# Layer 0's experts on tokens sorted by expert in DRAM, instead of every expert on every token

## The chip, the cores and the metric

The kernel runs on one NeuronCore of a Trainium2 chip. TensorE (PE) multiplies, VectorE (DVE), ScalarE (ACT) and GpSimd (POOL) work element by element, and SyncE (SP) issues nearly all DMAs. Every engine runs its own instructions in order, and waits for the others on semaphores. The metric is the device time in microseconds, lower is better.

## What is computed

A two-layer network on x of shape 16 batches x 256 tokens x 128 channels, all float32. Layer 0 is a recurrent mixer and an MLP, and then a mixture of 8 experts; layer 1 is an attention and then a mixture of 4 attention experts. Only layer 0's experts change:

```python
probs = softmax(x @ Wg)                      # 8 experts
top_vals, top_idx = top_k(probs, 2)          # two per token
top_vals = top_vals / sum(top_vals)
h = relu(einsum('ebsd,edh->ebsh', x * mask, W1) + b1)     # 128 -> 256
y = einsum('ebsh,ehd->ebsd', h, W2) + b2                  # 256 -> 128
out = sum(y * scores, axis=expert)           # scores are 0 but for two experts
x = layernorm(x + out)
```

## The kernel before

All engines walk the same list, `program_order()` (L272). First layer 0: 8 chunks of 512 tokens (two batches, 4 tiles of 128 rows), as steps (c, i) with i from 0 to 15. The chunks are pipelined by hand: in iteration c the mixer of chunk c+2, the MLP of chunk c+1 and the experts of chunk c run. Its iterations go from -2 to 8 (L276). Then follow the periods r of layer 1 with 24 slots each: -6 to 17 (L279). Periods -6, -5 and -4 hold only the projections and norms of the first batches (called the preparation here); from r = -3 (`EARLY_PERIODS`) the scores, maxima and exponentials of layer 1 start. Layer 1's large buffers lie over those of layer 0, so at (-3, 0) POOL, ACT and DVE wait until layer 0 has its last output (`x4_ready`, L961, L1079, L1356).

In layer 0's iteration c the work that matters here is, by the step's number:

- i = 0: DVE forms x1 of chunk c+1 (L561, L564) from the mixer's product; ACT sums its squares (L461), POOL takes the inverse root at i = 1 (L386, L388), DVE scales (L568, i = 2), PE transposes, ACT copies (i = 3).
- i = 4 to 9: the MLP of chunk c+1: PE multiplies by `wfc` (L698), ACT halves (L471), DVE takes the maximum (L611), ACT squares (L475), PE multiplies by `wmlp` (L704).
- i = 10 to 15: DVE adds and takes the norm's sums of chunk c+1 (L572 to L577), POOL the root, DVE writes x3 (L580, helper L518), PE transposes it and multiplies by `wg`. In between, the mixer of chunk c+2: transposes, k, v, the scan (L543), `wkv` (L547), the gate by exp, add, and two reciprocals (L551 to L554), `mixT` (L555), and PE's product with `wo0` (i = 15).
- i = 0 and 1: DVE picks the two best experts of each token of chunk c (L614 to L625).
- Experts, dense: each of the 8 on all 512 tokens. `hidden_at` and `output_at` place them: two products of 512 columns by `w1` (L650), ACT's relu with bias (L428), eight products of 128 columns by `w2` (L659), and DVE adds the output times the token's score (L596). All weights stay in SBUF.

A float32 product is two PE instructions in the trace; `mm` is the helper at L634.

SP loads everything at the start (`loads`, L370) and has no work in layer 0 after that. In layer 1 it issues small DMAs (`attention_sync`).

Of the kernel before, what the change touches and what calls it, by code (L numbers as in the profile page):

```python
# [28 lines left out]
STEPS, LAST_STEPS = 16, 6  # L29
# [22 lines left out]
class LayerZeroSignals:  # L52


    def __init__(self, sem):
# [11 lines left out]
        self.state_ready = sem("state_ready")  # L67
        self.mixT_ready = sem("mixT_ready")
        self.mix_ps = sem("mix_ps")
        self.mix_used = sem("mix_used")  # L70
# [18 lines left out]
        self.lg_copied = sem("lg_copied")  # L89
        self.lg_ready = sem("lg_ready")  # L90
        self.pexp_ready = sem("pexp_ready")
        self.score_ready = sem("score_ready")
        self.scoreT_ps = sem("scoreT_ps")
        self.scoreT_ready = sem("scoreT_ready")
        self.b2_ps = sem("b2_ps")
        self.b2_used = sem("b2_used")
        self.hidden_ps = sem("hidden_ps")
        self.hidden_ready = sem("hidden_ready")
        self.y_ps = sem("y_ps")
        self.y_used = sem("y_used")  # L100
        self.acc_sums = sem("acc_sums")
        self.acc_rstd = sem("acc_rstd")
        self.x4_ready = sem("x4_ready")
        self.dve_step = sem("dve_step")
        self.pool_step = sem("pool_step")
# [79 lines left out]
def program(nc, a, out):  # L185
    with ExitStack() as ctx:
# [8 lines left out]
        x4_all = sb("x4_all", [P, B * T, D])  # L195
# [26 lines left out]
        ew_ready = sem("ew_ready")  # L222
        exp_decay = sem("exp_decay")
        x_first = sem("x_first")
        x_loaded = sem("x_loaded")
# [4 lines left out]
        z = LayerZeroSignals(lambda name: sem(f"{name}_l0"))  # L230

# [40 lines left out]
        def program_order():  # L272

            for c in range(-2, CHUNKS + 1):  # L276
                for i in range(STEPS if c < CHUNKS else LAST_STEPS):
                    yield True, c, i
            for r in range(FIRST_PERIOD, B + 2):  # L279
                for i in range(SLOTS):  # L280
                    yield False, r, i

        with ExitStack() as ph:
            def sb0(name, shape, dt=F32):
# [7 lines left out]
            w1 = sb0("w1", [D, E0, HB * P])  # L292
            b1 = sb0("b1", [P, E0, HB])
            w2 = sb0("w2", [P, E0, HB, D])
            b2 = sb0("b2", [E0, D])
# [6 lines left out]
            x_all = sb0("x_all", [P, B * T, D])  # L302
# [3 lines left out]
            var0 = sb0("var0", [P, 4, CT])  # L306
            rstd0 = sb0("rstd0", [P, 4, CT])
            bn60 = sb0("bn60", [P, 2, CT, 6])
            mv0 = sb0("mv0", [P, 2, CT, 2])
# [4 lines left out]
            er = sb0("er", [D, CS])  # L314
# [10 lines left out]
            x3 = sb0("x3", [P, CT, D])  # L325
            acc = sb0("acc", [P, 2, CT, D])
            h_moe = sb0("h_moe", [P, 2, HB, CS])
            lg0 = sb0("lg0", [P, CT, E0])
            pr0 = sb0("pr0", [P, CT, E0])
            oh1 = sb0("oh1", [P, CT, E0])  # L330
            oh2 = sb0("oh2", [P, CT, E0])
            tk = sb0("tk", [P, CT, E0])
            st0 = sb0("st0", [P, 7, CT])
            score = sb0("score", [P, CT, E0])
            scoreT = sb0("scoreT", [E0, CS])
            hidden_bank = [ps[:, 0:2, :], ps[:, 2:4, :]]
            y_bank = [ps[:, 4, :], ps[:, 5, :]]
# [8 lines left out]
                (w1[:], a["w1"].rearrange("e i o -> i e o")), (b1[:], a["b1"].rearrange("e (c p) -> p e c", p=P)),  # L346
                (w2[:], a["w2"].rearrange("e (c p) d -> p e c d", p=P)), (b2[:], a["b2"]),
# [5 lines left out]
            def chunk(k):  # L353
                return 0 <= k < CHUNKS

            def hidden_at(c, i):

                if i % 2 == 0:
                    return None
                k, e = (c + 1, 0) if i == 15 else (c, (i + 1) // 2)  # L360
                return (k, e) if chunk(k) else None

            def output_at(c, i):

                if i % 2:
                    return None
                k, e = (c - 1, 7) if i == 0 else (c, i // 2 - 1)
                return (k, e) if chunk(k) else None

            def loads(sp):  # L370
# [4 lines left out]
                sp.dma_start(x_all[:, CT:B * T, :], x_rows[:, CT:B * T, :]).then_inc(x_loaded, DMA)  # L375
                for dst, src in loads0:
                    sp.dma_start(dst, src, allow_slow_non_contiguous=True).then_inc(loaded0, DMA)
# [1366 lines left out]
```

## Time and profile before

| | |
|---|---|
| median of 3 runs | 1551.77 us (1539.64 to 1557.17) |
| the profiled execution | 1544.68 us, its span 1542.9 us |
| PE, share of the span | 85% |
| DVE | 66% |
| ACT | 50% |
| POOL | 34% |
| mean granted clock of TensorE | 0.911 |

The span goes from the first instruction to the last. A busy share is a mean over stages that have different limits, so what one stage is worth is read from its own stretch. A gap is named by what ended it. The granted clock is a share of 2.4 GHz and has two levels, 1.2 and 2.4 GHz; a value between them is a mean over a stretch.

### The profile page before, as it was taken

The page shows a single profiled execution, that of the slowest core. Times are in us where ns is not written, and L with a number is a line of the kernel's source. Part 1 is how long each engine was busy: PE and PEld are TensorE (multiplying, and loading weights), DVE is VectorE, ACT ScalarE, POOL GpSimd, SP SyncE. Part 2 cuts the span into 40 slices and gives each one's busy share as a digit, 9 for nine tenths or more (in the row PEclk, how much of TensorE's full clock was granted, in tenths as well). Part 3 has the DMA queues.
Part 4 walks back from the last instruction along what each step waited for, and adds up shares of the span by engine and source line. Part 5 has one row for each costly group of instructions (what it writes and reads, how often), then busy time and mean ns, then how long its engine had stood idle before and what let it go on. Part 6 is the DMA issues. An engine that isn't in the chain of part 4 may idle for free.

```text
span 1542.9 us, 31463 instructions
## 1 busy us (share of the span) xinstructions
PE 1311.5 (85%) x12320; PEld 786.5 (51%) x12320; DVE 1017.0 (66%) x2422; ACT 767.9 (50%) x1260; POOL 525.6 (34%) x863
## 2 busy tenths in 40 slices
PE   4899999999655879889888899998989989988884
PEld 1566666667422335455445555555545545554543
DVE  3677667775444667777687777777777767757520
ACT  3334444433132356566465665665655656653540
POOL 1000010100342235346354454453544542442421
PEclk7999999999755879899899999999999999999986
DMA  7000000000000000101101011011010110110111
GB/s 206 1 1 1 1 1 1 0 1 1 0 1 9 9 2 9 38 11 33 31 13 42 18 26 37 8 42 31 13 42 5 39 36 9 42 36 10 32 34 36
DMA packets 34730, 35.03 MB, mean 23 GB/s; under 512 B 20070, under 2 KB 28440, under 8 KB 32536
## 3 DMA queue, kind: packets, MB, share of 16 engines
q1 hardware_dynamic: 34584, 33.03, 9.1%
q8 instruction: 99, 1.62, 0.5%
q14 instruction: 47, 0.39, 0.1%
HBM read 28.93 MB, written 2.88 MB: 21 GB/s over the span
## 4 chain that ended last, share of the span: by engine, by line
PE 44%; DVE 28%; SPq 7%; ACT 7%; POOL 5%; issue 5%; DMA 3%; DVEq 0%; ACTq 0%; POOLq 0%
PE ps L1367 17%; PE ps L634 14%; DVE mneg_e L1191 7%; PE ps L1445 7%; SPq L832 3%; PE ps L1468 3%; SPq L828 2%; DVE mneg_l L1191 2%; DVE acc L596 2%; DMA sums_l<-o_l 1%; SPq L850 1%; ACT probs L1038 1%; POOL q_low L915 1%; DMA sums_e<-o_e 1%; DVE equal L1217 1%
## 5 line engine op out<-in xcount | busy, mean ns | idle before, releaser
L1038 ACT ACTIVATE probs<-ps 128x1024 f32<-128x1024 f32 x384 | 389.8, 1024 | 244.9 <-PE ps L1367 243.9
L1191 DVE TENSOR_REDUCE mneg_e<-ps 128x2 f32<-128x512 f32 x512 | 337.1, 685 | 64.3 <-PE ps L1367 61.4
L1367 PE MATMUL ps<-k_high,q_high 32*128 32x256 f16 x1024 | 160.5, 283 | 50.6 <-DVE mneg_e L1191 41.3
L1191 DVE TENSOR_REDUCE mneg_l<-ps 128x2 f32<-128x512 f32 x256 | 167.8, 682 | 53.9 <-PE ps L1367 52.3
L1367 PE MATMUL ps<-q_high,k_high 32*128 32x256 f16 x1024 | 141.3, 276 | 4.1 <-ACT probs L1038 3.5
L1445 PE MATMUL ps<-probs,v_e 128*32 128x256 f32 x2048 | 138.6, 389 | 6.7 <-ACT v_e L1063 4.6
L1367 PE MATMUL ps<-q_low,k_high 32*128 32x256 f16 x1024 | 140.4, 273 | 0.0
L1367 PE MATMUL ps<-q_high,k_low 32*128 32x256 f16 x1024 | 139.6, 271 | 0.0
L428 ACT ACTIVATE h_moe<-ps,b 128x512 f32<-128x512 f32 x128 | 81.0, 684 | 116.9 <-PE ps L634 116.9
L634 PEld LDWEIGHTS ps<-w,h_moe 128*128 128x128 f32 x1024 | 122.1, 192 | 16.9 <-issue 16.7
L634 PE MATMUL ps<-w,h_moe 128*128 128x128 f32 x1024 | 124.6, 275 | 0.0
L634 PE MATMUL ps<-x3T,w 128*128 128x512 f32 x256 | 123.7, 606 | 0.0
L1367 PE MATMUL ps<-kT,qT 32*128 32x256 f16 x512 | 76.0, 290 | 33.2 <-DVE mneg_e L1191 17.0
L991 POOL TENSOR_TENSOR on_e<-o_e,on_e 128x512 f32<-128x512 f32 x64 | 80.6, 1272 | 62.5 <-DMA on_e<-scratch_e 62.5
L1367 PEld LDWEIGHTS ps<-k_high,q_high 32*128 32x128 f16 x1024 | 53.8, 93 | 93.9 <-DVE mneg_e L1191 62.1
L1246 DVE SCALAR_TENSOR_TENSOR q<-ps,bq,pick 128x256 f32<-128x256 f32 x128 | 55.6, 476 | 55.6 <-PE ps L1367 33.7
L1367 PE MATMUL ps<-wo,on_e 128*128 128x128 f32 x512 | 89.5, 346 | 0.0
L1367 PEld LDWEIGHTS ps<-q_high,k_high 32*128 32x128 f16 x1024 | 48.6, 93 | 77.4 <-issue 49.4
L921 POOL CAST k_high<-k 128x512 f16<-128x512 f32 x64 | 39.5, 618 | 139.0 <-ACT k L1054 139.0
L1367 PEld LDWEIGHTS ps<-wo,on_e 128*128 128x128 f32 x512 | 82.3, 252 | 4.5 <-issue 1.5
L1445 PEld LDWEIGHTS ps<-probs,v_e 128*32 128x32 f32 x2048 | 54.1, 110 | 58.6 <-issue 21.7
L1367 PE MATMUL ps<-x5T,wq 128*128 128x256 f32 x256 | 72.4, 405 | 5.7 <-ACT k L1054 4.9
(216 smaller groups left out, 2393.6 us busy)
## 6 DMA issues: line engine op xcount, KB each, us to landing
on_e<-scratch_e SPq DMA_DIRECT2D x64, 256.0 KB, 4.6
on_l<-scratch_l SPq DMA_DIRECT2D x128, 32.0 KB, 1.9
sums_l<-o_l SPq DMA_DIRECT2D x128, 2.0 KB, 1.7
q_high<-shiftT_e SPq DMA_DIRECT2D x128, 2.0 KB
sums_e<-o_e SPq DMA_DIRECT2D x128, 4.0 KB, 1.7
out<-y SPq DMA_DIRECT2D x16, 128.0 KB, 2.0
w<-in_w SPq DMA_DIRECT2D x1, 1024.0 KB
qT<-shiftT_l SPq DMA_DIRECT2D x64, 2.0 KB
```

The costliest lines, as they stand in the source:

```text
L428: last = act.activation(h_moe[:, e % 2, n, :], hidden_bank[e % 2][:, n, :], ACT.Relu, bias=b1[:, e, n:n + 1])
L596: last = v.scalar_tensor_tensor(acc[:, k % 2, t, :], y_bank[e % 2][:, t * D:(t + 1) * D], score[:, t, e:e + 1], base[:, t, :], ALU.mult, A ...
L634: return pe.matmul(o, l, r, start=start, stop=stop)
L832: sp.dma_start(sums_l[row:row + PACK, :], o_l[row:row + 1, :, :]).then_inc(L.sums_landed, DMA)
L921: pool.tensor_copy(k_high[:, b % 2, g], k32[:, g % 2]).then_inc(s.k16_ready, 1)
L991: pool.tensor_tensor(on_e[:, :, g], o_e[:, :, g], on_e[:, :, g], ALU.mult).then_inc(E.on_ready, 1)
L1038: act.activation(probs[:, probs_slot(r, i)].rearrange("p j s -> p (j s)"), s_banks(i).rearrange("p j s -> p (j s)"), ACT.Exp, scale=0.5 if ...
L1191: v.tensor_reduce(to, tiles(max_bank(k)), axis=AX, op=ALU.max, negate=True).then_inc(kind.max_used, 1)
L1246: last = v.scalar_tensor_tensor(q32[:, g % 2, c, :], x0[:, c * S:(c + 1) * S], bq[:, c, g:g + 1], pick[:, c, :], ALU.add, ALU.mult)
L1367: return pe.matmul(o, l, r, start=start, stop=stop)
L1445: last = pe.matmul(x1[ROW * j:ROW * (j + 1), to * S:(to + 1) * S], values, probs[:, probs_slot(r, first + 2 * t + j // 2), j % 2, c * S:(c ...
L1468: last = pe.matmul(x0[:, c * S:(c + 1) * S], wk[:, c, g, :], x5T[:, b % 2], start=False, stop=True, skip_group_check=True)
```

## The change

Layer 0 is cut into two groups of 4 chunks. The router's choice is turned into a place: a mask of the two chosen experts is multiplied on PE with a triangle of ones (rank within the tile) and with all ones (count of the tile), and DVE adds these to running first rows. POOL then writes every row of x3 twice, by indirect DMA with 128 row numbers, into `by_expert[g]` in DRAM, which has a region for each expert. When a group is complete, DVE makes a table of 40 tiles: first row, and first row of the expert's weights. The experts run over these in 10 quads of 4 tiles. For every tile SP reads row numbers from the table into registers, loads 128 tokens and all of the expert's weights and biases (642 values for each of 128 rows), and stores the 128 outputs over the tokens. Later POOL gathers each token's two outputs, by two indirect DMAs per tile, and DVE adds them to x3 with their shares, and normalizes.

Group 0's quads lie in iterations 4 to 7; group 1's lie after layer 0, beside the preparation and the sums of group 0. The sums of group 1 lie on the odd slots from r = -3 on. DRAM regions are zeroed at the start. Besides this, the gate is a tanh on ACT and one DVE instruction; the mixer's and the MLP's scales are multiplied into the weights once; x1 + x is formed on POOL. The core of the diff:

```diff
-            for c in range(-2, CHUNKS + 1):
-                for i in range(STEPS if c < CHUNKS else LAST_STEPS):
-                    yield True, c, i
-            for r in range(FIRST_PERIOD, B + 2):
+            experts_at = {(4, 8), (4, 13), (5, 2), (5, 7), (5, 12), (6, 2), (6, 7), (6, 12), (7, 1), (7, 5), (7, 9), (7, 13)}
+            n = -1
+            for c in range(-2, CHUNKS):
+                for i in range(STEPS):
+                    yield "layer0", c, i
+                    if (c, i) in experts_at:
+                        yield "experts", 0, n
+                        n += 1
+            prepared = [("attention", r, i) for r in range(FIRST_PERIOD, EARLY_PERIODS) for i in range(SLOTS)]
+            summed = list(sums_of(0))
+            done = 0
+            for n in range(-1, QUADS + 1):
+                yield "experts", 1, n
+                yield from summed[3 * (n + 1):3 * (n + 2)]
+                upto = len(prepared) * max(n, 0) // QUADS
+                yield from prepared[done:upto]
+                done = upto
+            rest = sums_of(1)
+            for r in range(EARLY_PERIODS, B + 2):
                 for i in range(SLOTS):
-                    yield False, r, i
+                    yield "attention", r, i
+                    if i % 2:
+                        yield from itertools.islice(rest, 1)
...
+                sp.wait_ge(set_up, 1)
+                for g in range(GROUPS):
+                    if g > 0:
+                        sp.wait_ge(z.filled, DMA * FILLS * g)
+                    rows_of_group = by_expert[g].rearrange("(p n r) d -> n p (r d)", p=P, n=FILLS)
+                    for n in range(FILLS):
+                        sp.dma_start(rows_of_group[n], zeros).then_inc(z.filled, DMA)
...
+                    if i in (10, 12, 13, 14) and chunk(c):
+                        t = (10, 12, 13, 14).index(i)
...
+                        for n in range(2):
+                            pool.indirect_dma_start(by_expert[g], bass.IndirectOffsetOnAxis(ap=places[:, n, at:at + 1], axis=0),
+                                                    x_all[:, at, :], None).then_inc(z.scattered[g], DMA)
...
+                        for n in range(2):
+                            pool.indirect_dma_start(gathered[:, k % 2, n, t, :], None, by_expert[g],
+                                                    bass.IndirectOffsetOnAxis(ap=places[:, n, k * CT + t:k * CT + t + 1], axis=0))\
+                                .then_inc(ex.gathered[k % 2], DMA)
...
-                    link(v.tensor_scalar(gate[:], er[:], 1.0, None, ALU.add))
-                    link(v.reciprocal(gate[:, 0:S], gate[:, 0:S]))
-                if i == 14 and chunk(k):
-                    link(v.reciprocal(gate[:, S:CS], gate[:, S:CS]))
-                    v.tensor_tensor(mixT[:], wkv[:], gate[:], ALU.mult).then_inc(z.mixT_ready, 1)
+                        v.scalar_tensor_tensor(mixT[:], gate[:], 1.0, wkv[:], ALU.add, ALU.mult).then_inc(z.mixT_ready, 1)
...
+                    if n + 1 < QUADS:
+                        q = QUADS * g + n + 1
+                        take(5, ex.tokens_ready, q + 1)
+                        pe.wait_ge(ex.tokens_loaded[q % 3], DMA * QUAD * (q // 3 + 1))
+                        for j in range(QUAD):
+                            last = pe.transpose(tokens_bank[:, j * P:(j + 1) * P], tokens[:, q % 3, j, :], ident[:])
...
+                        pe.wait_ge(ex.tokens_ready, q + 1)
+                        pe.wait_ge(ex.weights_loaded[q % 3], DMA * QUAD * (q // 3 + 1))
+                        for j in range(QUAD):
+                            for k in range(HB):
+                                last = pe.matmul(hidden_bank[q % 2][:, k, j * P:(j + 1) * P], expert_w[:, q % 3, j, k * P:(k + 1) * P],
+                                                 tokensT[:, q % 2, j * P:(j + 1) * P], start=True, stop=True)
...
+                    if n >= 1:
+                        q = QUADS * g + n - 1
+                        take(4, ex.out_ready, q + 1)
+                        pe.wait_ge(ex.hidden_ready, q + 1)
...
+                def load_weights(g, n):
+                    q = QUADS * g + n
+                    if q > 2:
+                        sp.wait_ge(ex.out_ready, q - 2)
+                    for j, row in enumerate(values(g, 1, n)):
+                        sp.dma_start(expert_w[:, q % 3, j, :], a["expert_w"][bass.ds(row, P), :]).then_inc(ex.weights_loaded[q % 3], DMA)
+                def slot(g, n):
+                    if n == -1:
+                        sp.wait_ge(z.filled, DMA * FILLS * GROUPS)
+                        sp.wait_ge(z.table_ready, g + 1)
+                        load_weights(g, 0)
+                        sp.wait_ge(z.scattered[g], DMA * 2 * CT * GROUP_CHUNKS)
+                        for ahead in range(2):
+                            load_tokens(g, ahead)
+                        load_weights(g, 1)
+                    if n >= 1:
+                        store_outputs(g, n - 1)
+                    if 0 <= n < QUADS - 2:
+                        load_tokens(g, n + 2)
+                    if 0 <= n < QUADS - 2:
+                        load_weights(g, n + 2)
...
+                        for n in range(2):
+                            add = v.scalar_tensor_tensor(x_all[:, token, :], gathered[:, k % 2, n, t, :], shares[:, n, token:token + 1],
+                                                         x_all[:, token, :], ALU.mult, ALU.add)
+                            link(add)
...
                     if (r, i) == (EARLY_PERIODS, 0):
-                        v.wait_ge(z.x4_ready, CHUNKS)
+                        for n in range(2):
+                            v.wait_ge(ex.stored[n], DMA * QUAD * QUADS)
```

In slot n PE transposes the tokens of quad n + 1, makes the hidden product of quad n (8 products of 128 columns) and the output product of quad n - 1 (8 more). ACT copies the transposed tokens and takes 8 relus of 128 columns; DVE adds the bias of the outputs (4 instructions) and signals `out_ready`. `load_tokens` and `store_outputs` on SP are made as `load_weights`: four row numbers read into registers, four DMAs; the store waits for `out_ready` of its quad. In the sums, POOL waits for `ex.stored` (all stores of the group) before the first gather, and DVE for `ex.gathered`.

## Rows read from the trace of the kernel before

**Rows 1.** The page: span, busy time, PE and its clock in 40 slices.

```profile
span 1542.9 us, 31463 instructions
...
PE 1311.5 (85%) x12320; PEld 786.5 (51%) x12320; DVE 1017.0 (66%) x2422; ACT 767.9 (50%) x1260; POOL 525.6 (34%) x863
...
PE   4899999999655879889888899998989989988884
...
PEclk7999999999755879899899999999999999999986
```

**Rows 2.** Groups in layer 0 (0 to 420 us): busy us, mean ns.

```profile
L634 PE MATMUL ps<-w,h_moe 128*128 128x128 f32 x1024 | 124.6, 275 | 0.0
L634 PE MATMUL ps<-x3T,w 128*128 128x512 f32 x256 | 123.7, 606 | 0.0
...
L428 ACT ACTIVATE h_moe<-ps,b 128x512 f32<-128x512 f32 x128 | 81.0, 684 | 116.9 <-PE ps L634 116.9
L596 DVE SCALAR_TENSOR_TENSOR acc<-ps,score,acc 128x128 f32<-128x128 f32 x224 | 62.8, 343 | 12.8 <-PE ps L634 12.0
```

**Rows 3.** Timeline, iterations -2 and -1: start us, us, engine, work.

```profile
20.92 2.04 PE L634 MATMUL ps<-wo,mixT 128*128 128x128 f32 x8 [6.44 <-DVE mixT L555]
...
23.73 0.69 DVE L564 TENSOR_TENSOR x_sb<-tmp,x_all 128x512 f32<-128x512 f32 x1
...
39.04 3.81 PE L634 MATMUL ps<-wmlp,h_fc 128*128 128x128 f32 x32 [2.79 <-ACT h_fc L475]
...
49.05 1.11 DVE L518 TENSOR_SCALAR x<-tmp,mv,rstd 128x128 f32<-128x128 f32 x4
...
50.53 1.75 DVE L552 RECIPROCAL gate<-gate 128x256 f32<-128x256 f32 x1
...
51.70 1.85 PE L634 MATMUL ps<-wg,x3T 128*128 128x8 f32 x8 [0.77 <-ACT x3T L478]
...
59.47 0.69 DVE L564 TENSOR_TENSOR x_sb<-tmp,x_all 128x512 f32<-128x512 f32 x1
```

**Rows 4.** Timeline of iteration 2, with dense experts.

```profile
149.86 0.69 DVE L564 TENSOR_TENSOR x_sb<-tmp,x_all 128x512 f32<-128x512 f32 x1
...
152.13 1.95 PE L634 MATMUL ps<-w,h_moe 128*128 128x128 f32 x16
...
156.75 0.63 PE L638 MATMUL ps<-ident,xn 128*128 128x128 f32 x4 [0.95 <-DVE xn L568]
```

**Rows 5.** Timeline of DVE: x1 of chunk 5 begins iteration 4.

```profile
241.36 0.69 DVE L564 TENSOR_TENSOR x_sb<-tmp,x_all 128x512 f32<-128x512 f32 x1
```

**Rows 6.** DMA GB/s, 40 slices of 0 to 60 us; issues on SP.

```profile
GB/s 0 168 200 41 250 291 307 291 298 287 339 240 30 206 395 411 322 369 382 281 198 0 0 0 0 0 0 0 0 0 0 0 0 5 0 0 0 11 5 0
...
0.73 0.44 SPq L372 DMA_DIRECT2D x_all<-in_x  x1
...
452.75 2.69 SPq L884 DMA_DIRECT2D qT<-shiftT_l  x4
```

**Rows 7.** The page's DMA issues: KB each, us to landing.

```profile
sums_l<-o_l SPq DMA_DIRECT2D x128, 2.0 KB, 1.7
```

**Rows 8.** Timeline of POOL: the root, and slots (-3, 0), (-3, 21), (-2, 21).

```profile
404.39 1.01 POOL L388 TENSOR_TENSOR rstd<-var,half 128x4 f32<-128x4 f32 x1
...
437.57 2.66 POOL L962 MEMSET v_e<- 128x3072 f32 x1
...
455.87 0.72 POOL L996 TENSOR_TENSOR x_all<-x_all,bproj 128x256 f32<-128x256 f32 x1
...
496.18 0.72 POOL L996 TENSOR_TENSOR x_all<-x_all,bproj 128x256 f32<-128x256 f32 x1
```

**Rows 9.** Stretch, length, busy us of PE, PEld, DVE, ACT, POOL; clock, DMA.

```profile
404.00:437.00 33.00, 10.32 (x33) 4.58 (x34) 13.75 (x28) 6.45 (x12) 19.20 (x52) 0.54 0.00 0
...
437.00:458.00 21.00, 13.76 (x60) 4.49 (x58) 13.05 (x23) 4.75 (x9) 9.38 (x21) 0.50 0.00 1
458.00:498.00 40.00, 22.40 (x154) 8.93 (x154) 14.44 (x30) 13.28 (x20) 9.52 (x23) 0.59 0.04 8
```

More of the change, by code:

```diff
@@ L1 @@
+import itertools
 import numpy as np
@@ L576, in slot @@
-                        link(v.tensor_tensor(tmp[:], tmp[:], rows(x_all, k), ALU.add))
-                        sums(0, tmp).then_inc(z.x3_sums, 1)
+                        for t in range(CT):
+                            last = v.bn_stats(bn60[:, t, :], tmp[:, t, :])
+                        link(last)
+                        for t in range(CT):
+                            last = v.bn_aggr(mv0[:, t, :], bn60[:, t, :])
+                        last.then_inc(z.x3_sums, 1)
                     if i == 12 and chunk(k):
@@ L626, in slot @@
-                    if i == 2 and chunk(c - 1):
-                        sums(1, acc[:, (c - 1) % 2]).then_inc(z.acc_sums, 1)
+                        if c == 0:
+                            v.wait_ge(const_ready, 7)
+                        first_largest(pr0[:], st0[:, 3, :], chosen[:, 0])
+                    if i == 1 and chunk(c):
+                        link(v.scalar_tensor_tensor(lg0[:], chosen[:, 0], -2.0, pr0[:], ALU.mult, ALU.add))
+                        first_largest(lg0[:], st0[:, 4, :], chosen[:, 1])
+                        v.tensor_tensor(mask[:], chosen[:, 0], chosen[:, 1], ALU.add).then_inc(z.mask_ready, 1)
@@ new lines, in layer0_vector, with experts_vector, slot @@
+                return slot
+            def experts_vector(v):
+                def slot(g, n):
+                    if n >= 1:
+                        q = QUADS * g + n - 1
+                        v.wait_ge(ex.out_ps, q + 1)
+                        if q > 1:
+                            v.wait_ge(ex.stored[q % 2], DMA * QUAD * (q // 2))
+                        for j in range(QUAD):
+                            b2 = expert_w[:, q % 3, j, EXPERT_COLS - D:EXPERT_COLS]
+                            last = v.tensor_tensor(y_tokens[:, q % 2, j, :], out_bank[:, j * D:(j + 1) * D], b2, ALU.add)
+                        last.then_inc(ex.out_ready, 1)
+                return slot
@@ L1078, in slot @@
                     if (r, i) == (EARLY_PERIODS, 0):
-                        act.wait_ge(z.x4_ready, CHUNKS)
+                        for n in range(2):
+                            act.wait_ge(ex.stored[n], DMA * QUAD * QUADS)
                         act.wait_ge(values_ready, 1)
@@ L1611, in _ @@
                 loads(sp)
-                step = attention_sync(sp)
-                for in_layer0, r, i in program_order():
-                    if not in_layer0:
-                        step(r, i)
+                experts, attention = experts_sync(sp), attention_sync(sp)
+                for part, r, i in program_order():
+                    if part == "experts":
+                        experts(r, i)
+                    if part == "attention":
+                        attention(r, i)
                 for p in range(2):
```

534 lines of the change are left out of this document (341 added, 193 removed).

## The prediction

> **What bounds the kernel now.** I read the page's slices first: PE is busy nine tenths in nearly all of the first ten slices, at the full clock, then falls to five or six tenths for about three, with the clock in between [rows 1]. So layer 0 is bound by PE, and behind it lies a stretch that nothing fills. The groups of layer 0 say what PE does: the experts' two products take 124.6 + 123.7 = 248 us, and ACT's relus and DVE's score sums stand beside them with 81.0 and 62.8 us [rows 2]. The timeline gives the beat: x1 of chunk 3 at 149.86 and of chunk 5 at 241.36, so 45.75 us for an iteration [rows 4, 5]. The busy times by stretch show the rest: the preparation of layer 1, 404 to 437 us, has 10.32 us of PE in 33 us at a mean clock of 0.54; r = -3 has 13.76 in 21 us, and r = -2 22.40 in 40 us, both near the lower level [rows 9]. These are chains of single steps through all engines, where added work on one engine is paid in part even though it looks idle. From -2 on nothing of the kernel changes.
>
> **Iterations without experts.** The trace holds one: iteration -1, x1 at 23.73 and the next at 59.47, 35.7 us [rows 3]. In it the product with `wg` ends at 53.55, 29.8 us after its start; only then come dense experts and a late `mixT`. In the new kernel the mixer's product can follow at once: 29.8 + 2.04 (that product at the low clock) + 0.2 of handoffs, less about 0.5 for the two adds of DVE that go, plus 0.5 for the choice and the places, which wait beside ACT's squares and PE's `wmlp` product (3.81 us): 32 us. The reciprocals (1.75 each) are off this path but for the first chunk, where they and one add fall out: its x1 comes at 23.73 - 3.9 - 0.7 = 19.1. Five such iterations (-1 to 3) end at 19 + 160 = 179, where the kernel before is at 241.4 [rows 3, 5]. That is a gain of 62 us, the surest of the terms. A tanh in place of an exp on ACT is priced as the same.
>
> **Group 0's experts.** A tile needs the two products once instead of for 8 experts on 32 tiles: 80 tiles instead of 256, 31% of PE's 248 us. For a quad of 4 tiles: 16 instructions hidden and 16 out, 1.95 us each, and 0.63 for transposes, 4.5 us at the full clock [rows 4]; at the low one 8 instructions take 2.04 instead of half of 1.95, so 8.9 us [rows 3, 4]. One quad in three fits into the gap before the transposes at i = 3. At i = 7 the eight relus (an estimate of 0.3 us each, from 0.684 for 512 columns [rows 2]) stand on ACT before the last square of the MLP: 1.95 + 2.4 + 0.2 = 4.6 us. At i = 12, 2 us. So iteration 4 takes 34.5, iteration 5 39, iteration 6 34 (it has no mixer), together to 287. Iteration 7 has neither mixer nor MLP and holds four slots of quads, so it takes the quads' own beat.
>
> **The quads' beat q.** For a quad SP reads 12 row numbers and issues 12 DMAs, one after another, and behind each wait for `out_ready` stands everything that SP has to do. Let u be SP's time for one read and one issue. Three weight buffers make a loop over two quads: after `out_ready` 12u of SP (the weights come last), about 3 us to land, the hidden and the output product (3.8 each at the low clock), 1.2 of DVE and its handoff. So q is the larger of 12u and 6u + 5.6. The bytes do not bind: 1.3 MB of weights and 0.5 MB of tokens at the 300 to 400 GB/s of the first loads [rows 6] are 5 to 6 us.
>
> The issue costs 0.44, in layer 1 2.69/4 = 0.67 [rows 6]. No row shows a register read. Bounds: nothing, so u = 0.44; or a round trip like that of the smallest DMA, 1.7 us [rows 7], for each, so u = 2.4. I take one such round trip for four reads in a row, since four stand together, and an issue between the two rows: 0.55 + 0.42 = 0.95. Then q = 11.4.
>
> The Trainium skill (DMA: Bandwidth & Descriptors, section Latency and other measured facts) gives a register load from memory a floor of about 600 ns and says that compilers unroll four of them. No run here shows it. By it u would be an estimated 0.70 if four overlap (q = 9.8, the sum about 23 us lower) or 1.15 if they don't (q = 13.8, about 32 us higher).
>
> **From iteration 7 to (-3, 0).** 3q of slots and 5 us for the last output: 292 + 3q. Then, on SP in order: the last store, weights and tokens of group 1's first quad, 12u, and 4.5 us to land, transpose and copy: the first hidden product at 296.5 + 3q + 12u. (The scatters of the last chunk, 8 on POOL, come about then too and are taken as hidden.) Nine more quads 9q; then product, relus, product, bias 11 us, the store 4u, landing 2: 309.5 + 12q + 16u = 309.5 + 136.8 + 15.2 = 461.5. There ACT, DVE and POOL pass their wait. Before, POOL is there at 437.57 [rows 8]. So 24 us are lost, although 62 were won before iteration 4: the preparation's 33 us are hidden under this phase, but group 1's ten quads stand after layer 0 and cost 114. (In the kernel before, nothing of the experts is left there.) PE is then so thin that its clock will stay low.
>
> **Group 1's sums.** From (-3, 1) on every odd slot holds a step: 12 in r = -3, 9 in r = -2. The period r = -3 takes 21 us now, r = -2 40 us [rows 8, 9]. In r = -3 POOL gets 24 indirect DMAs, and DVE 8 steps of two linked sums (0.343 [rows 2], and an estimated 0.25 for the link), twice the norm's sums (1.3 each, estimated) and one scaling (1.11 [rows 3]): 9.4 + 2.6 + 1.1 = 13 us. Let P be one indirect DMA on POOL. No row shows one; bounds 0.44 as on SP [rows 6] and 1.7 as for a whole round trip [rows 7]. I take 1.1, by POOL's root, 1.01 us [rows 8]. POOL then has 9.38 + 26.4 + 2.5 = 38 us in a period of 21: +17; r = -2, with 8 gathers and much slack, +5. Together +22 (with P = 0.5 POOL has 24 and DVE 26: +8; with P = 1.7, +36).
>
> The sum: 1544.7 + 24 + 22 = 1591. It is made against the profiled execution's own time, 1544.68, which lies 7 us under the median of 1551.77; I leave the 7 us out and predict 1590, 2.5% above the median.
>
> **Where costs are put at nothing.** The zeros, 17.8 MB at 300 GB/s, 60 us, end before the second iteration's end and hold only the first scatters; if they are slower than 200 GB/s, POOL's root at i = 11 waits behind a scatter. Eight scatters in an iteration lie beside PE's `wmlp` product and the kv chain as long as P is under 1.8. The constants on POOL, the folding of the scales and DVE's tables are a few microseconds beside idle stretches.
>
> **Rivals.**
> 1. SP is cheap and PE and its chain set the beat: u = 0.5, q = 7.8 (4.5 of PE at the full clock and 33/10 of preparation), P = 0.5. Then 309.5 + 93.6 + 8 = 411, 26 us gained, 8 lost: 1527, faster. For it speaks SP's single issue of 0.44 [rows 6]; against it that each value is also read, and the low clock in that stretch [rows 9]. It decides from u below about 0.55 with the full clock.
> 2. Reads or gathers cost more than I take: u = 1.3 gives q = 15.6, so 309.5 + 187.2 + 20.8 = 517.5 and 15 more in iterations 5 and 6, with +22: 1662. For it speaks SP's 0.67 in layer 1 [rows 6] before any read.
> 3. In layer 0 PE's share falls from nine tenths to about four, and the clock stays at the lower level, as in r = -3, where 13.76 of 21 us gave 0.50 [rows 9]. The MLP's product then takes 7.6 instead of 3.81, the others 2.5 more: 38 us an iteration, 30 more in five: 1620. Against it: iteration -1 ran its `wmlp` product at the full clock after the low one of 20.92 [rows 3].
> 4. Partly cheap: u = 0.7 and P = 0.6 give 309.5 + 117.6 + 11.2 = 438 and +10: 1556, within 1%.
>
> A sentence of the skill speaks against the change as a whole: the same page, section Bandwidth, calls transfers under 64 KB bound by descriptors; the scattered and gathered tiles are of 64 KB in rows of 512 bytes. In this trace the first loads in such rows reached some 300 GB/s [rows 6], so I give bytes no part in the sum.
>
> **How the numbers follow.** The forecast (1565 to 1610) 0.37; rival 1 0.18; rival 2 0.17; rival 3 0.08; rival 4 0.20. The range goes from 1525 (rival 1) to 1660 (just short of rival 2). Faster by over 1% (under 1536, about what a measurement can tell): 0.18. Within 1%: 0.20. Slower: 0.62.
>
> **What would show it.** Right: x1 of chunk 5 at about 179; SP busy or issuing without pause from iteration 4 to -3, quads of group 1 11 us apart, PE's gaps there ended by DMAs of weights or tokens; POOL at (-3, 0) near 460; r = -3 near 38 us, with POOL's gaps gone. Wrong: quads 8 us apart with PE's waits ended by ACT or DVE (rival 1), iterations of 38 us at clock 0.5 (rival 3), or POOL's indirect DMAs far off 1.1.

## The result

The changed kernel takes 1672.86 us (median of 4 runs, 1668.46 to 1674.06) where the kernel before takes 1553.82 (4 runs on the same chip, 1539.64 to 1557.17). The ratio is 1.078, with a 95% interval from 1.071 to 1.085: slower by 7 to 8.5%, as the sign of the forecast said, but 83 us above its 1590 and outside its range. The profiled execution took 1668.46 us, its span 1666.7. Times below are medians of all executions of a run, while ratios leave out the only one that fell into the chip's slower state (of the run with dense experts and the rest of the change).

The page of the kernel after: span, busy time, PE and its clock in 40 slices of 41.7 us.

```profile
span 1666.7 us, 31540 instructions
...
PE 1239.0 (74%) x11696; PEld 752.1 (45%) x11696; DVE 957.1 (57%) x2305; ACT 738.7 (44%) x1304; POOL 664.7 (40%) x1082
...
PE   4665675534344468889999889999988889899883
...
PEclk7767788765767557789999999999989999999887
```

PE has 72 us less to do, DVE 60 us less [rows 1], and the span is 124 us longer. PE's nine tenths of the first ten slices are gone. From slice 16 on the digits look as they did; what was lost lies ahead of that.

Timeline of DVE after: x1 of chunk 0, x1 of chunk 5, and the bias step of some quads (one row is four instructions).

```profile
17.98 0.69 DVE L703 TENSOR_TENSOR x_sb<-ps,x_all 128x512 f32<-128x512 f32 x1 [1.31 <-PE ps L820]
...
191.77 0.69 DVE L703 TENSOR_TENSOR x_sb<-ps,x_all 128x512 f32<-128x512 f32 x1 [1.49 <-PE ps L820]
...
358.28 0.89 DVE L779 TENSOR_TENSOR y_tokens<-ps,expert_w 128x128 f32<-128x128 f32 x4 [3.82 <-PE ps L925]
401.85 0.89 DVE L779 TENSOR_TENSOR y_tokens<-ps,expert_w 128x128 f32<-128x128 f32 x4 [22.99 <-PE ps L925]
...
517.51 0.88 DVE L779 TENSOR_TENSOR y_tokens<-ps,expert_w 128x128 f32<-128x128 f32 x4 [14.96 <-PE ps L925]
```

Timeline of POOL after: (-3, 0), and the ends of periods -3 and -2 (their slot 21).

```profile
532.22 2.65 POOL L1207 MEMSET v_e<- 128x3072 f32 x1
...
570.07 0.74 POOL L1241 TENSOR_TENSOR x_all<-x_all,bproj 128x256 f32<-128x256 f32 x1
...
614.81 0.72 POOL L1241 TENSOR_TENSOR x_all<-x_all,bproj 128x256 f32<-128x256 f32 x1
```

Read the marks one after another. Chunk 5's x1 comes at 191.77, before it was 241.36 [rows 5]: 50 us are won. At 358.28 group 0's last quad gets its bias. The first quad of group 1 follows only at 401.85, and from there the quads are 16.5 us apart on the mean (the seven steps from 401.85 to 517.51 are 115.7 us; the last two are 4.2 and 3.3). POOL reaches (-3, 0) at 532.22, before at 437.57 [rows 8]: 94.7 us lost, where the forecast had 24. From that mark to the end of the span it was 1105.3 us and is 1134.5, 29 more, where the forecast had 22. So of the 78 us that the sum (1591, against 1668.46) missed, 71 lie ahead of (-3, 0).

### The profile page after: what moved, and what is told of

Read it like the earlier page. It is cut to its first block, busy times and chain, and to the rows that moved or that the text cites. A ratio compares the mean times of both kernels' runs of the same rounds, so it can differ in the third digit from the quotient of the medians.

```text
span 1666.7 us, 31540 instructions
## 1 busy us (share of the span) xinstructions
PE 1239.0 (74%) x11696; PEld 752.1 (45%) x11696; DVE 957.1 (57%) x2305; ACT 738.7 (44%) x1304; POOL 664.7 (40%) x1082
## 4 chain that ended last, share of the span: by engine, by line
PE 40%; DVE 22%; SPq 11%; issue 8%; ACT 8%; POOL 6%; DMA 4%; another core or an unknown queue 0%; DVEq 0%; ACTq 0%; POOLq 0%
PE ps L1614 16%; DVE mneg_e L1437 7%; PE ps L1692 7%; PE ps L820 6%; PE ps L916 3%; PE ps L1715 3%; SPq L1076 3%; SPq L935 2%; DVE mneg_l L1437 2%; PE ps L925 2%; DMA tokens<-by_expert 2%; SPq L957 2%; SPq L1072 2%; SPq L944 1%; DMA sums_l<-o_l 1%
## 5 line engine op out<-in xcount | busy, mean ns | idle before, releaser
L906 PE MATMUL ps<-ident,tokens 128*128 128x128 f32 x80 | 20.3, 404 | 129.7 <-DMA tokens<-by_expert 127.2
L779 DVE TENSOR_TENSOR y_tokens<-ps,expert_w 128x128 f32<-128x128 f32 x80 | 17.7, 283 | 166.8 <-PE ps L925 161.8
L509 POOL DMA_INDIRECT by_expert<-x_all,places x64 | 63.6, 994 | 110.3 <-DVE places L762 94.0
L1230 POOL CAST routeT<-routeT 21x256 f16<-21x256 f32 x16 | 6.2, 386 | 180.7 <-ACT routeT L1368 180.7
L1692 PE MATMUL ps<-probs,v_l 128*32 128x256 f32 x1024 | 77.0, 423 | 1.1 <-DVE qkv L1505 0.3
```

The lines of the kernel that those rows point to most:

```text
L509: pool.indirect_dma_start(by_expert[g], bass.IndirectOffsetOnAxis(ap=places[:, n, at:at + 1], axis=0), x_all[:, at, :], None).then_inc(z.s ...
L1692: last = pe.matmul(x1[ROW * j:ROW * (j + 1), to * S:(to + 1) * S], values, probs[:, probs_slot(r, first + 2 * t + j // 2), j % 2, c * S:(c ...
```

## Why the quads are 16.5 us apart

The chain of waits of the kernel after, from the bias step of one quad to that of the next (start us, us, what ends later; L935 is the reading of the row numbers on SP).

```profile
436.91 0.89 DVE y_tokens L779 x4
437.82 0.30 SPq L935
...
439.33 0.35 SPq L957
...
441.31 0.30 SPq L935
...
442.82 0.35 SPq L944
...
444.41 1.81 DMA tokens<-by_expert
446.35 1.09 PE ps L906 x4
447.44 3.41 PE ps L916 x16
450.86 2.18 PE ps L925 x16
453.11 0.89 DVE y_tokens L779 x4
```

Nothing in it is long, and nothing in it overlaps. When quad n - 1 has its bias, SP reads four row numbers and stores (until 441.3), reads four more and issues the tokens of quad n + 2 (until 444.4): 6.6 us. They land in 1.8. PE transposes them (1.09), and only behind these transposes stand, in PE's order, the hidden product of quad n + 1 (3.41) and the output product of quad n (2.18). Then DVE gives n its bias (0.9), and SP may go on. That is 16.2 us from one quad to the very next, however many buffers the tokens have: the buffers allow quad n + 2 to be loaded long before, but the store of n - 1 stands ahead of its loads on SP. Waits of 400 to 526 us say the same:

```profile
DVE y_tokens L779 <- PE ps L925: 99.9, 9, 23.0
...
PE ps L906 <- DMA tokens<-by_expert: 58.7, 7, 11.2
```

The prediction had a loop over two quads through the three weight buffers, and this loop it did not see.

## Experiments

### Tokens ahead of the store

```
-                    if n >= 1:
-                        store_outputs(g, n - 1)
                     if 0 <= n < QUADS - 2:
                         load_tokens(g, n + 2)
+                    if n >= 1:
+                        store_outputs(g, n - 1)
```

> SP loads the tokens of quad n+2 before it stores the outputs of quad n-1; nothing else moves. Theory (a one-quad loop: the store and the tokens stand on SP behind out_ready of quad n-1, and PE's output product of quad n stands behind the transposes of quad n+2's tokens, so each quad pays SP 7 us + landing 2 + PE 7 + DVE 1): the quads of group 1 come 10 to 12 us apart instead of 16.5, and the time falls by 70 to 100 us, to about 1590. Rival A (SP's 12 reads and issues are the limit as such): 10.4 us busy a quad, so no less than that, indistinguishable below 11 us. Rival B (weights or DMA bandwidth bind): the quads stay above 14 us apart and the time falls by less than 30 us.

Measured: 1614.63 us (1607.23 to 1621.02), 1.037 of the kernel before, interval 1.030 to 1.044; 58 us less than the change. Timeline of SP, three quads of group 1:

```profile
413.57 3.28 SPq L957 DMA_DIRECT2D by_expert<-y_tokens  x4
418.42 1.92 SPq L951 DMA_DIRECT2D expert_w<-in_expert_w  x4
421.91 1.88 SPq L944 DMA_DIRECT2D tokens<-by_expert  x4
425.36 1.93 SPq L957 DMA_DIRECT2D by_expert<-y_tokens  x4
...
436.34 1.93 SPq L957 DMA_DIRECT2D by_expert<-y_tokens  x4
```

In this stretch SP goes without a pause: a group of four DMAs takes 1.9 us, the four reads ahead of it 1.55, so 12 of each are 10.4 us, and the stores are 11.8 and 11.0 apart. Earlier it still pauses, by 2.7 us ahead of the weights of 393.69. The seven steps from 371.29 to 453.69 have 11.8 us on the mean, which is near the beat of the prediction (11.4), with a different loop taken away first. The one-quad loop is shown: two lines in another order, no work less, and POOL is at (-3, 0) at 471.43 instead of 532.22, 60.8 us earlier. The beat is the one expected, the gain in time (58 us) is less than the 70 to 100 expected; 13 us of the difference lie behind (-3, 0), in the profiled execution (1147.8 us to the end, where the change took 1134.5).

### No reads on SP

`values` gives constants in place of the table's entries, so the tiles hold other rows and experts than the routing's, and the output isn't the reference's. The number and the size of all transfers stay.

```
-                    return nc.values_load_multi_w_load_instructions(
-                        tile_table[0:1, g, kind, q * QUAD:(q + 1) * QUAD], engines=[mybir.EngineType.SP],
-                        min_val=0, max_val=(SORTED_ROWS - P, (E0 - 1) * P)[kind])[1]
+                    return [(q * QUAD + j) * P if kind == 0 else ((q * QUAD + j) // 5) * P for j in range(QUAD)]
```

> The changed kernel with constant row numbers instead of values read from the table: SyncE reads nothing, and issues the same 12 DMAs a quad with the same sizes (the table's content is left out, so the experts work on other rows and weights). It measures what reading costs. By the profile of the changed kernel a group of four takes 1.9 us of issue and 1.55 us between the groups; 8 of the 12 reads are in the one-quad loop, so 16.5 - 3.1 = 13.4 us a quad, and the time falls by about 50 us. If the pause between groups is not the read but the wait on a semaphore or the queue, it stays at 16 us.

Measured: 1608.6 us, one run. Timeline of SP:

```profile
404.23 1.75 SPq L955 DMA_DIRECT2D by_expert<-y_tokens  x4
406.02 1.85 SPq L942 DMA_DIRECT2D tokens<-by_expert  x4
407.92 1.85 SPq L949 DMA_DIRECT2D expert_w<-in_expert_w  x4
417.38 1.75 SPq L955 DMA_DIRECT2D by_expert<-y_tokens  x4
```

The groups follow each other after 0.04 us instead of 1.55. Eight reads fall out of the chain, 3.1 us, and the beat falls from 16.5 to 13.4 (seven steps from 363.33 to 457.16): the loop is still there, with 7.6 us of pause in it for SP (409.8 to 417.4). In group 1's beat the order costs more (16.5 to 11.8) than the reads (16.5 to 13.4); in the whole the two edits are alike, with POOL at (-3, 0) at 471.43 and 471.89, since without reads the gap between the groups is shorter as well (363.33 - 331.16 = 32 us instead of 43.6).

### Both, and POOL's add later: what the sorted kernel could reach

The two edits above and the one of the run "POOL's add later" below. The output isn't the reference's, for the same reason.

> Sorted experts with everything found so far taken away from SP: tokens issued ahead of the store, row numbers as constants in the code (the table is not read, so the tiles hold other rows and experts than the right ones and the output is not the reference's), and POOL's add after x1's transposes. Theory (SP and the loop through it set the quads' beat): 12 issues of 0.45 us are 5.4 us, then the weights' loop over two quads, 5.4 of SP, 3 to land, 3.8 to 5 of products, 1.2 of DVE, gives 7 to 7.5; PE's own chain at the low clock is 8.9, so quads 9 us apart instead of 10.7 to 12, 18 us less over ten quads, 10 less between the groups, 6 to 8 less in layer 0: 1614.6 - 35 = 1580. Rival (bytes or PE's chain at the low clock already set 10.7 to 12): quads stay at 10.5 or more and the time at 1595 to 1605. Neither comes down to the kernel before, 1553, since the ten quads of group 1 still stand after layer 0.

Measured: 1573.22 us (1564.90 to 1576.93), 1.011 of the kernel before (1.003 to 1.019). Timeline of DVE (three quads of group 1) and of POOL, (-3, 0) and the end of period -3:

```profile
400.46 0.88 DVE L779 TENSOR_TENSOR y_tokens<-ps,expert_w 128x128 f32<-128x128 f32 x4 [7.07 <-PE ps L925]
404.42 0.89 DVE L779 TENSOR_TENSOR y_tokens<-ps,expert_w 128x128 f32<-128x128 f32 x4 [1.01 <-PE ps L925]
417.30 0.88 DVE L779 TENSOR_TENSOR y_tokens<-ps,expert_w 128x128 f32<-128x128 f32 x4 [8.15 <-PE ps L925]
...
432.00 2.66 POOL L1205 MEMSET v_e<- 128x3072 f32 x1
...
469.93 0.73 POOL L1239 TENSOR_TENSOR x_all<-x_all,bproj 128x256 f32<-128x256 f32 x1
```

The first quad of group 1 gets its bias at 343.31, 28 us earlier than with tokens first alone, but the quads are still 10.6 us apart on the mean (seven steps to 417.30), long and short ones in turn. That beat is the one of the on-record rival, 10.5 or more, though the time is below the forecast of both. One wait of 6.09 us is for tokens:

```profile
410.69 1.09 PE L906 MATMUL ps<-ident,tokens 128*128 128x128 f32 x4 [6.09 <-DMA tokens<-by_expert]
```

These tokens were issued from 405.07 to 406.92, behind the 1.3 MB of weights issued at 403.17, and PE gets them 3.8 us after the last issue, not 1.8. So bytes can count once SP is cheap. But they are not all. The step from 343.31 to 357.08 ends when DVE has waited for POOL to zero layer 1's buffers (until 356.0), and the one from 385.87 to 400.46 goes through the norm of group 0's sums (DVE to 389.5, POOL to 390.9) and then the preparation's product on PE (392.55), behind which the next transposes stand (394.2). So the work laid beside the quads sets some of the long steps. What PE's low clock costs here was not told apart.

POOL is at (-3, 0) at 432.00, 5.6 us before the kernel before. But period -3 takes 37.9 us where it took 18.3, from (-3, 0) to the end it is 1137.9 us where it was 1105.3, and the kernel before is not reached: the interval lies above 1, if by little. With a cheap SP the change just pays for group 1 and then loses on the sums, which rival 1 had at 8.

### Weights on ACT's queue

Group 1's weights are read and issued by ACT instead of SP; tokens ahead of the store; POOL's gathers of group 0 wait until group 1 has its first hidden product; the sums of group 1 on every fourth slot from r = -2.

```
+                    if g == 1 and 0 <= n < QUADS - 2:
+                        load_weights(g, n + 2)
```

> As e1 with late gathers and spread sums, and group 1's weights are read and issued by ScalarE's queue. SyncE then has 8 of the 12 reads and issues: 7 us a quad. If SyncE is what bounds e1's quads (10.7 us), they come 8 to 9 us apart and the time is about 1565 to 1580; if the two-quad loop through the weights binds, 10 us and 1590. In neither case does it reach the kernel before.

Measured: 1595.54 us (1591.13 to 1605.87), 1.030 of the kernel before (1.021 to 1.039), and 19 us under the run with tokens first. POOL is at (-3, 0) at 455.32 instead of 471.43. The first quad of group 1 gets its bias at 360.49 instead of 371.29, and from there the quads are 11.4 us apart (seven steps to 440.60) instead of 11.8 (371.29 to 453.69). Neither expectation came true (8 to 9 us and 1565 to 1580, or 10 and 1590). Against the run with the same late gathers ("Gathers of group 0 later", 12.0 us a quad, (-3, 0) at 475.41) it is 0.6 us a quad and 20 us at (-3, 0). So taking a third of SP's work away moves the beat little: it was not SP alone that set it. The trace shows what else did. POOL's gathers of group 0, held back until 347.57, push its zeroing for layer 1 back until 376.5, DVE waits for that, and the second quad gets its bias 17.1 us after the first (377.58); and beside the gathers that follow on POOL, SP's pieces take 0.70 us again (379.8 to 387, 392.3 to 399). It is the fastest sorted kernel of the series that computes the whole result, and still the slower one.

### POOL's add later

```
-                    if i == 3 and chunk(c + 1):
-                        pool.wait_ge(z.x1_ready, c + 2)
+                    if i == 5 and chunk(c + 1):
+                        pool.wait_ge(z.x1T_ps, c + 2)
```

> The changed kernel with GpSimd's add x1 + x two steps later (after PE's transposes instead of beside VectorE's scaling of x1). If the add holds VectorE up, the four scalings take 0.9 us again instead of 1.9, and an iteration of layer 0 33.2 instead of 34.2 us. Otherwise neither moves.

Timeline of POOL and DVE in iteration 1 of the kernel after, and of DVE in this run:

```profile
92.63 1.25 POOL L497 TENSOR_TENSOR xx<-x_sb,x_all 128x512 f32<-128x512 f32 x1
92.67 1.88 DVE L711 TENSOR_SCALAR xn<-x_sb,rstd 128x128 f32<-128x128 f32 x4 [0.16 <-POOL rstd L452]
```

```profile
90.99 0.88 DVE L711 TENSOR_SCALAR xn<-x_sb,rstd 128x128 f32<-128x128 f32 x4 [0.16 <-POOL rstd L452]
```

Measured: 1653.52 us, one run, 15 under the profiled execution of the change (1668.46). The four scalings take 0.88 us again, the iterations from chunk 1's x1 to chunk 5's 33.0 us instead of 34.1 (54.83 to 186.67), and (-3, 0) comes at 523.04 instead of 532.22. So the add that the change moved to POOL, where the prediction counted only that two adds of DVE go, costs 1.0 to 1.1 us in each iteration, through DVE.

### The rest of the change with dense experts

The kernel before, with the new parts that have nothing to do with sorting: a tanh for the gate, the norm scales folded into the weights, the add of x1 and x on POOL.

```
-                        act.activation(er[:], x0, ACT.Exp, scale=-1.0).then_inc(z.er_ready, 1)
+                        act.activation(gate[:], x0, ACT.Tanh, scale=0.5).then_inc(z.er_ready, 1)
-                        link(v.tensor_scalar(gate[:], er[:], 1.0, None, ALU.add))
-                        link(v.reciprocal(gate[:, 0:S], gate[:, 0:S]))
+                        v.scalar_tensor_tensor(mixT[:], gate[:], 1.0, wkv[:], ALU.add, ALU.mult).then_inc(z.mixT_ready, 1)
```

> The kernel before with only what the change did besides the experts: tanh gate, scales multiplied into the weights, x1 + x on GpSimd. Dense experts stay. If PE is the bound of layer 0, only the start (first x1 about 5.7 us earlier) and about 1 us an iteration of waits for VectorE are gained: 8 to 18 us less than before, ratio 0.99 to 0.995. If the long stops of VectorE's reciprocals were on the path: 25 us or more.

Measured: 1538.62 us (1524.43 to 1555.83), 0.984 of the kernel before, interval 0.976 to 0.992; by the medians it is 0.990. It beats both kernels, the one before by 1 to 1.6%. x1 of chunks 2 to 4 is 44.7 us apart (103.10, 147.81, 192.51) where it was 45.75, and (-3, 0) comes at 432.14 instead of 437.57. Of the 15 us of the medians 5.4 stand at (-3, 0); the rest lies in the later periods, where nothing was changed. So what is good in the change is not the sorting, and the sorting alone costs more than the 119 us that the two kernels are apart: 1672.86 - 1538.62 = 134.

### Dense, with the late add

The same with the edit of "POOL's add later".

> Dense experts with the tanh gate, the folded scales and the add of x1 and x on POOL, as in the dense run before, but POOL adds only after x1's transposes. If DVE's scaling of x1 (four instructions at 1.88 us beside POOL's add, 0.88 alone) lies on the path of a dense iteration, it saves up to 1 us in each of 8 iterations: 8 us below that run's 1538.6, so 1531. If PE's product sets the iteration there (124 + 124 us of experts' products), the change is nothing: 1538, and a late add can even hold the MLP's output.

Measured: 1539.14 us (10 runs, 1530.31 to 1546.85), 0.990 of the kernel before (0.986 to 0.994). The iteration is 43.8 (100.12, 143.90, 187.67), and (-3, 0) comes at 423.70, 8.4 us before the run without the late add, just as expected. PE's products are the same, and still the iteration is 2.0 us shorter than in the kernel before: layer 0 was not bound by PE alone. But the end doesn't move (1531 was expected): from (-3, 0) to the end it is 1113.0 us here, 1108.3 there, 1105.3 in the kernel before, and the two intervals lie over each other. A gain of 8 us at (-3, 0) is about what the later periods vary by.

### The sums: half of the gathers

Group 1 gathers its first output alone; its second term is what group 0 left in the buffer, so the output isn't the reference's.

```
-                        for n in range(2):
+                        for n in range(2 - g):
                             pool.indirect_dma_start(gathered[:, k % 2, n, t, :], None, by_expert[g],
```

> In group 1 each token gathers only the first of its two outputs (32 indirect DMAs of 64 are left out there; VectorE still does both sums, one with an old value). If GpSimd's 1.26 us for each bounds period -3, that period falls from 38 us by 15, and the time by 15 to 20 us. If VectorE's 8 steps bound it, less than 5 us.

Measured: 1666.04 us, one run, against 1668.46. Timelines of POOL, the kernel after in r = -3, then this run's (-3, 0) and its ends of periods -3 and -2:

```profile
545.74 0.95 POOL L526 DMA_INDIRECT gathered<-by_expert,places  x1 [0.31 <-issue]
546.99 0.94 POOL L526 DMA_INDIRECT gathered<-by_expert,places  x1 [0.30 <-issue]
```

```profile
531.18 2.66 POOL L1207 MEMSET v_e<- 128x3072 f32 x1
...
561.49 0.73 POOL L1241 TENSOR_TENSOR x_all<-x_all,bproj 128x256 f32<-128x256 f32 x1
...
604.14 0.72 POOL L1241 TENSOR_TENSOR x_all<-x_all,bproj 128x256 f32<-128x256 f32 x1
```

A gather takes POOL 0.95 us and a pause of 0.30, so 1.25. Period -3 falls from 37.9 to 30.3 and -2 from 44.7 to 42.7: POOL's gathers have a part in r = -3, as predicted. But it falls by half of the 15 us that 12 gathers are worth, and the end gains only 2.4. Where the rest went, to DVE's linked sums, which stayed, or to the variation of the later periods, one run doesn't tell.

### The sums: spread over later periods

Tokens ahead of the store, and group 1's steps on every fourth slot from r = -2.

```
-                    if i % 2:
+                    if i % 4 == 3 and r >= -2:
```

> As e1 (tokens loaded before the store), and the 21 steps of group 1's sums lie on every fourth slot from r = -2 on instead of on every second slot from r = -3 on. In e1 the periods -3 to -1 take 134 us against 107 before. If the crowding of GpSimd's gathers in r = -3 and -2 is the cost, r = -3 goes back to about 18 us and the whole falls by 10 to 20 us against e1, since a gather of 1.26 us finds room in later periods. If every step costs its VectorE time wherever it stands, the sum of the periods -3 to 1 stays as in e1 within 5 us.

Measured: 1631.79 us, one run, where tokens first alone has 1614.63. Period -3 is back to 18.3 us, as in the kernel before. But -2 takes 44.5, -1 58.6, 0 66.5, 1 68.8, where the run with tokens first has 44.7, 51.5 and 58.2 for -2 to 0. From (-3, 0) to the end of r = 1 that is 256.7 us against 253.7, within the 5 us of the second expectation. So the steps cost about the same wherever they stand, and no stretch was found that takes them for nothing, not even the one that looked empty [rows 9]. The rest of the 17 us between the two times lies elsewhere, and one run says nothing of it: in the run with the weights on ACT, whose sums are spread in the same way, -3 to 1 take 255.8 us and the rest 880.5, where this run has 901.1.

### Gathers of group 0 later

```
+                            if g == 0:
+                                pool.wait_ge(ex.hidden_ps, QUADS + 1)
```

This stands beside tokens ahead of the store, too. It asks where the gap between the groups (358.28 to 401.85) comes from. In it SP is slow. POOL and the chain of waits of the kernel after:

```profile
365.98 1.00 POOL L526 DMA_INDIRECT gathered<-by_expert,places  x1 [6.23 <-DMA by_expert<-y_tokens]
...
375.82 0.69 issue
376.51 0.70 SPq L944
...
380.74 0.70 SPq L935
...
387.04 0.70 issue
```

POOL's 16 gathers go from 365.98 to 385.7 without a break, and for the last ten of these microseconds each piece on SP, a read, an issue or what lies between, takes 0.70 us.

> As e1, and GpSimd begins the gathers of group 0 only after the first hidden product of group 1. In e1 and in the changed kernel SyncE needs 10 us between the first tokens and the next weights of group 1, 0.70 us for each of its instructions, while GpSimd issues 16 gathers back to back. If the gathers slow SyncE, that gap falls to 2 us, and the first outputs of group 1 come about 8 us earlier. If it is a property of the place in the program, the gap stays at 10 us.

Measured: 1618.31 us, one run, against 1614.63 without this edit: nothing gained, where 8 us at the first output were expected. Timeline of SP:

```profile
338.04 5.67 SPq L946 DMA_DIRECT2D tokens<-by_expert  x8
345.27 1.88 SPq L953 DMA_DIRECT2D expert_w<-in_expert_w  x4
...
356.40 4.25 SPq L946 DMA_DIRECT2D tokens<-by_expert  x4
```

The pause between tokens and weights falls from 10.5 us (377.2 to 387.7 in the kernel after) to 1.6, so the slow stretch does come with POOL's 16 gathers. But it comes back where these now stand, from 356 on, and the first quad of group 1 gets its bias at 373.41 instead of 371.29. For SP the reads are part of it as well: without them the same gathers, back to back, leave SP at full pace.

The slow stretch isn't SP's alone. PE and ACT of the kernel after, the first hidden product of group 1 and its relus:

```profile
378.71 3.62 PE L916 MATMUL ps<-tokensT,expert_w 128*128 128x128 f32 x16
...
388.57 2.17 ACT L611 ACTIVATE h_moe<-ps,expert_w 128x128 f32<-128x128 f32 x8 [9.03 <-remote]
```

The product ends at 382.3 and the relus begin 6.2 us later, 2.9 us behind POOL's last gather of the sixteen; nothing that the trace shows ends this wait. In the run without reads they begin 9.5 us after the product (347.7 to 357.16), and with the ideal SP 10.1 (327.1 to 337.14), again 1 to 3 us behind the last gather. In the two runs that hold the gathers back they follow within 0.1 us. With the late gathers it is PE that slows down where these now stand: the hidden product of 363.48 takes its first eight instructions in steps of 0.70 us or a multiple of it, and is done at 375.4, 11.9 us after its start, where the one above takes 3.6. So back to back gathers on POOL held up SP, ACT and PE in turn, and constants in place of reads helped only SP. Why was not found out.

## Point by point

**Direction and bound: right.** PE's 248 us of dense products were cheap to have, since they hid everything else; group 1's quads and its sums stand alone behind layer 0.

**An iteration without experts: 32 us predicted, 34.1 measured** (chunk 1's x1 at 55.52, chunk 5's at 191.77: 136.25 over four; the first, from 17.98, took 37.5). POOL's add is 1.1 of it. The MLP's product took 5.44 us in all five (-1 to 3), not 3.81, with the clock at 0.67 to 0.76 in windows of 50 us between 50 and 200: rival 3 in a small form, by 1.6 us an iteration instead of 6. Together 12.8 us late at chunk 5.

**SP's time for one read and issue, u: 0.95 predicted, 0.87 measured** (10.4/12). Right, and by parts too: the issue 0.48, the read 0.39 (predicted 0.55 and 0.42, which add up to 0.97 and not to the 0.95 used; with 0.97 the sum would be 3 us higher). The Trainium skill (DMA: Bandwidth & Descriptors, Latency and other measured facts) has a floor of about 600 ns for a load; the chain shows 0.30 us for the first of four and 0.15 for each of the others, so here its 0.70 (four that overlap) would have been too low for u and its 1.15 too high.

**The step that failed: "q is the larger of 12u and 6u + 5.6".** It rests on "Three weight buffers make a loop over two quads". The loop that bound goes through the tokens and over one quad: 8 reads and 8 issues on SP (6.6), landing 1.8, transposes 1.1, hidden 3.4, out 2.2, bias 0.9, so 16.2 against 11.4. The swap of the two SP lines took 60.8 us at (-3, 0) out of the 94.7 lost and left it 9.9 above the forecast's 461.5. The trace of before could not show it, but the code did: `store_outputs(g, n - 1)` waits for `out_ready` and stands ahead of `load_tokens(g, n + 2)`, and the transposes of n + 2 stand ahead of the output product of n. The prediction had itself written that behind each wait for `out_ready` stands everything that SP has to do, and then followed only the weights. With q = 16.5 and u = 0.87, the prediction's 309.5 + 12q + 16u is 521.4, and with the 12.8 from layer 0 it is 534.2, against 532.22 measured. That it fits so well has luck in it: in iterations 5 and 6 the quads' beat ruled as well (bias steps from 231.28 to 346.99, 16.5 apart), which the sum did not have, and the last two quads of each group, whose loads are out early, take 3.3 to 6.6 us, so that the nine steps of group 1 are 123.2 us and not 148.5.

**Between the groups: 15.9 us predicted from the last bias to the first hidden product, 19.5 measured** (359.2 to 378.7). The 12u of SP was in it. The last chunk's scatters, called hidden, run from 349.75 to 359.75; SP does not wait for them, but while they run its pieces take up to 0.70 us. From the first hidden product to (-3, 0) it is 153.5 us instead of 119.4. Of these 34.1 us, 13.0 lie ahead of the first bias (24.0 us for product, relus, product and bias instead of 11), because the output product stands behind the transposes of quad 2, whose tokens SP issues only at 391.38, behind its slow stretch of about 9 us; 20.6 in the nine steps of the quads (123.2 instead of 9q = 102.6), 0.5 in the end. Against the forecast's own marks the 70.7 us at (-3, 0) are then: 12.8 up to chunk 5, 20.2 up to group 0's last quad (359.2 - 191.8 against 147.2), 3.6 in the gap, 34.1 in group 1.

**The sums: +22 predicted, +29 measured.** P is 1.25 against 1.1. Period -3, from (-3, 0) to its slot 21, takes 37.9 us instead of 18.3, so 19.6 more (17 predicted); -2 takes 4.4 more (5 predicted), -1 3.4, 0 and 1 together 2.2 less, and 4 lie behind. These 29 us are known only roughly: in the other runs with the same steps after (-3, 0), from there to the end takes 1128.7 to 1147.8 us, where the change has 1134.5.

**Rivals.** Rival 2 (1662) came nearest to the time, for a wrong reason: its q of 15.6 came from u = 1.3. Rival 1's cheap SP was tried, and even so the kernel was 1.1% slower than before; its cheap gathers (P = 0.5) are not what the chip has. Rival 4 wanted u = 0.7 and P = 0.6, measured are 0.87 and 1.25.

## What to carry to other kernels

To price a loop over several engines, don't stop at the buffers: list for each queue what stands ahead of each load in the order in which it is issued, and follow the wait at its head; a load that has a free buffer but stands behind a store of the last result is as late as that store. Work taken off the busiest engine is worth nothing in a stretch whose length is then set by another chain, and what it leaves behind the main loop is paid in full. When a change has several parts, time the small ones alone: here they won 1 to 1.6% while the whole lost 7.8%.

## What the runs showed of the hardware

- Four reads of row numbers with their bounds took SP 1.55 us, 0.30 for the first read and 0.15 for each other; four issues took 1.9.
- While POOL issued its gathers back to back, the pieces on SP took 0.70 us each, where they take 0.04 to 0.35 otherwise; with constants in place of the reads this was gone on SP, but ACT's relus still began only 1 to 3 us after the last gather, 9.5 to 10.1 us after their product.
- An indirect DMA of 128 rows kept POOL for 0.95 us, with 0.30 to the next.
- POOL's add of 128x512 (1.25 us) beside DVE's four scalings took DVE from 0.88 to 1.88 us. The Trainium skill (SBUF — State Buffer, section SBUF: two separate sides) tells of an exclusive lock on a shared pair of ports, which GpSimd, or DVE in a mode that uses two ports, holds for a whole instruction. The 1.00 us lost beside an add of 1.25 agrees; in which mode the scalings run is shown by no run here.
